# Normalised tiles in halves over both PSUM banks, with scale, shift and the first MLP matmul in units of their own

## The reference

```
def block(x, cond):                       # six times: attn, mlp, mlp, mlp, attn, mlp
    xn = (x - mean) * rsqrt(var + eps)    # over 128 features
    xm = xn * scale(cond) + shift(cond)
    y = attention(xm)  or  gelu(xm @ W1 + b1) @ W2
    return x + gate(cond) * (y + bias)
```

## Time and profile before

| | us |
|---|---|
| median of 3 runs | 586.82 (585.61 to 589.59) |
| profiled execution, whole | 584.34 |
| profiled execution, span from first to last instruction | 582.6 |
| PE busy in the span | 490.1 |
| DVE busy | 460.5 |
| ACT busy | 367.5 |
| POOL busy | 316.2 |

### The profile page before, as it was taken

One profiled execution on the slowest core, in us unless ns is written; L12 is line 12 of the kernel. 1 busy time (PEld: TensorE's weight loads), 2 busy tenths in 40 slices (PEclk: granted clock), 3 DMA queues, 4 the chain that ended last, 5 costly groups with the idle time before them and its releaser, 6 DMA issues.

```text
span 582.6 us, 23163 instructions
## 1 busy us (share of the span) xinstructions
PE 490.1 (84%) x10086; PEld 340.5 (58%) x10086; DVE 460.5 (79%) x1091; ACT 367.5 (63%) x598; POOL 316.2 (54%) x326
## 2 busy tenths in 40 slices
PE   4798658879889889689999898756889999887997
PEld 1465545656466565556667566544658666565755
DVE  5689798987886657989989876769988677899941
ACT  5865325754596759758868656522577468966652
POOL 4877356643463654685676546444353767834150
PEclk9989868898799896999999999675999999997899
DMA  8723411240232432525425413130132344422130
GB/s 293 304 89 100 125 24 35 48 120 3 74 94 60 123 96 85 135 76 151 124 78 136 105 31 84 37 98 4 24 95 72 84 128 118 115 59 61 50 97 37
DMA packets 40117, 53.51 MB, mean 92 GB/s; under 512 B 5840, under 2 KB 30672, under 8 KB 40016
## 3 DMA queue, kind: packets, MB, share of 16 engines
q1 hardware_dynamic: 39552, 51.14, 31.1%
q10 hardware_dynamic: 432, 0.88, 0.4%
q0 software_dynamic: 32, 0.01, 0.3%
HBM read 39.68 MB, written 2.88 MB: 73 GB/s over the span
## 4 chain that ended last, share of the span: by engine, by line
PE 48%; DVE 23%; issue 11%; POOL 10%; ACT 6%; DMA 1%; ACTq 0%; POOLq 0%; DVEq 0%
PE work L1067 10%; PE work L1058 10%; PE work L1009 8%; PE work L1024 6%; PE work L973 4%; DVE prob L862 3%; DVE stats L886 3%; PE work L976 3%; POOL xm L644 2%; PE work L981 2%; DVE mx L854 2%; DVE work L905 2%; POOL rstd L637 2%; DVE x L908 2%; DVE prob L856 2%
## 5 line engine op out<-in xcount | busy, mean ns | idle before, releaser
L736 ACT ACTIVATE xn<-x,nmr,rstd 128x128 f32<-128x128 f32 x192 | 79.0, 486 | 41.6 <-POOL nmr L639 41.4
L1058 PE MATMUL work<-xm,w_layer 128*128 128x512 f32 x176 | 94.9, 659 | 6.6 <-POOL xm L644 5.1
L1009 PE MATMUL work<-kbd,qT 32*32 32x80 f32 (+1 forms) x4096 | 73.6, 270 | 24.7 <-issue 17.2
L741 ACT ACTIVATE prob<-work,first 128x512 f32<-128x512 f32 x88 | 59.0, 686 | 50.5 <-PE work L1058 50.4
L727 ACT ACTIVATE prob<-prob 128x640 f32<-128x640 f32 (+1 forms) x64 | 57.5, 898 | 50.2 <-POOL prob L629 39.0
L1067 PEld LDWEIGHTS work<-w_layer,prob 128*128 128x128 f32 x704 | 82.0, 193 | 11.7 <-ACT prob L741 8.8
L1067 PE MATMUL work<-w_layer,prob 128*128 128x128 f32 x704 | 85.6, 279 | 3.0 <-ACT prob L741 2.9
L637 POOL TENSOR_TENSOR rstd<-veps,neg_half 128x4 f32<-128x4 f32 x48 | 48.9, 1018 | 66.2 <-DVE veps L893 66.2
L1009 PEld LDWEIGHTS work<-kbd,qT 32*32 32x32 f32 x4096 | 59.2, 110 | 42.7 <-issue 30.2
L644 POOL TENSOR_TENSOR xm<-turned_in,mod 128x512 f32<-128x512 f32 x48 | 50.7, 1058 | 54.5 <-DVE turned_in L899 54.5
L862 DVE STREAM_TRANSPOSE prob<-prob 128x1024 f32<-128x1024 f32 x64 | 77.2, 1227 | 2.5 <-ACT prob L727 2.5
(11 more groups left out here) (128 smaller groups left out, 828.6 us busy)
## 6 DMA issues: line engine op xcount, KB each, us to landing
gate<-gates SPq DMA_DIRECT2D x192, 128.0 KB, 3.3
vbd<-v_ev SPq DMA_DIRECT2D x128, 72.0 KB, 2.5
kbd<-in_adj SPq DMA_DIRECT2D x8, 704.0 KB, 6.5
turned_in<-in_x_tok SPq DMA_DIRECT2D x8, 256.0 KB, 2.9
out_x<-x SPq DMA_DIRECT2D x8, 256.0 KB, 2.1
turned_in<-in_x_feat SPq DMA_DIRECT2D x7, 256.0 KB, 4.6
w_layer<-in_weights SPq DMA_DIRECT2D x2, 768.0 KB, 14.2
prob<-in_modw SPq DMA_DIRECT2D x1, 768.0 KB, 10.9
```

Of the source, the lines that this page charges most:

```text
L736: act.activation(xn[s][:, t], x[s][:, t], ACT.Identity, scale=rstd[s][:, t:t + 1], bias=nmr[s][:, t:t + 1]).then_inc(xn_ready[s], 1)
L741: act.activation(hT[s][u], bank(s, f"h{j}.{u}"), GELU[BLOCKS[j][3]], bias=vec(HID_BIAS[j], u)).then_inc(h_ready[s], 1)
L1009: last = pe.matmul(to[:, b * GH * n:(b + 1) * GH * n], qT[s][rows_g, q * S:(q + 1) * S], kbd[s][rows_g, :, q * n:(q + 1) * n], start=(a != ...
L1058: pe.matmul(bank(s, f"h{j}.{u}"), w[UP[j]][:, 0, u * D:(u + 1) * D], xm[s][:], start=True, stop=True).then_inc(filled[s], 1)
```

## The change

HALVES = 2. The stages norm and modulate of a block become two each, numbered 2j and 2j + 1. The ACT part of a norm half makes two tiles, the PE part transposes two tiles into the first 256 columns of a bank of its own (fills xnj.0 and xnj.1, which lie in different banks of the stream, and turn the parity of the fills behind them). DVE scales 256 columns and POOL shifts 256 columns per half, with semaphores that count twice as far. The first hidden unit of an MLP block is two matmuls of 256 columns into one bank, each waiting for its half; the other units are whole. The attention's keys stage waits for both halves. What is computed is the same. All five MERGE strings are new: 48 more entries on PE, DVE, ACT and POOL, and the same number on SP. Of the strings, the first line of PE's stands here for all.

```diff
--- before.py
+++ after.py
@@ -77,6 +77,7 @@
 OUT_BIAS = ["L1_cond_bproj", "L1_cond_b2", "L2_cond_ssm_b2", "L2_cond_ff_b2", "L3_cond_proj_b", "L3_cond_fc2_b"]
 NATT = 4
 UNITS = 4
+HALVES = 2
 
 
 def by_pair(kind, a):
@@ -90,7 +91,9 @@
               ("self_out", 0),
               *by_pair("turn", 1), *by_pair("values", 1), ("divide", 1), ("graph_sum", 0), ("graph_out", 0)]
     for j, (kind, _, hidden, _) in enumerate(BLOCKS):
-        stages += [("stats", j), ("norm", j), ("modulate", j)]
+        stages += [("stats", j)]
+        for k in range(HALVES):
+            stages += [("norm", HALVES * j + k), ("modulate", HALVES * j + k)]
         if kind == "attn":
             a = ATTN_OF_BLOCK[j]
             stages += [("keys", a), ("base", j), ("vals", a), ("scores", a * PAIRS), ("softmax", a * PAIRS), ("scores", a * PAIRS + 1),
@@ -118,7 +121,7 @@
         ahead = [(*st, c + NS) for st in EDGES]
         at = own.index(("stats", NBLK - 1, c)) + 1
         own[at:at] = ahead
-        own.insert(own.index(("modulate", NBLK - 1, c)) + 1, ("next_x", 0, c))
+        own.insert(own.index(("modulate", HALVES * NBLK - 1, c)) + 1, ("next_x", 0, c))
     else:
         own.remove(("next_adj", 0, c))
     return own
@@ -150,24 +153,25 @@
     return [next(turns[int(s)]) for s in merge]
 
 MERGE = {
-    "tensor": ("001014414042420420132021030023021022201210212122011212121230230023023132323013113203022223321003"
...
+    "tensor": ("010104401404402104120310032132010131031200213103031330231030332322022112223333003010131222233210"
...
 }
 ORDERS = {engine: order(engine, merge) for engine, merge in MERGE.items()}
 
@@ -176,7 +180,7 @@
     names = ["rs", "self", "q a0", "k a0", "v a0", "S0 a0", "S1 a0", "q a1", "k a1", "v a1", "O0 a0", "O1 a0", "S0 a1", "S1 a1",
              "selfT", "O0 a1", "O1 a1"]
     for j, (kind, _, hidden, _) in enumerate(BLOCKS):
-        names.append(f"xn{j}")
+        names += [f"xn{j}.{k}" for k in range(HALVES)]
         if kind == "attn":
             a = ATTN_OF_BLOCK[j]
             names += [f"q a{a}", f"k a{a}", f"v a{a}", f"S0 a{a}", f"S1 a{a}", f"O0 a{a}", f"O1 a{a}", f"oT a{a}"]
@@ -400,6 +404,9 @@
         def by_seq(a):
             return a.rearrange("p (q n) -> p q n", n=S)
 
+        def half_seqs(a, k):
+            return by_seq(a)[:, k * NB // HALVES:(k + 1) * NB // HALVES]
+
         def keys_order(a):
             return a.rearrange("p (b t n) -> p t b n", b=BT, t=T)
 
@@ -433,7 +440,8 @@
         for j_, a_ in ATTN_OF_BLOCK.items():
             READ[f"oT a{a_}"] = (oT_ready, 2, a_ - 1)
         for j_ in range(NBLK):
-            READ[f"xn{j_}"] = (scaled, NBLK, j_ + 1)
+            for k_ in range(HALVES):
+                READ[f"xn{j_}.{k_}"] = (scaled, HALVES * NBLK, HALVES * j_ + k_ + 1)
             READ[f"y{j_}"] = (x_ready, NBLK + 1, j_ + 2)
             for u_ in range(BLOCKS[j_][2]):
                 READ[f"h{j_}.{u_}"] = (h_ready, NHID, HIDDEN_BEFORE[j_] + u_ + 1)
@@ -552,7 +560,7 @@
                     sp.wait_ge(scored[s], count(c, NATT * PAIRS, NATT * PAIRS))
                     load_adj(c + NS)
                 if kind == "next_x":
-                    sp.wait_ge(xm_ready[s], count(c, NBLK, NBLK))
+                    sp.wait_ge(xm_ready[s], count(c, 2 * NBLK, 2 * NBLK))
                     load_x(c + NS)
                 if kind == "store":
                     await_x(sp, c, NBLK)
@@ -638,10 +646,13 @@
                     pool.wait_ge(rstd_ready[s], count(c, 2 * NBLK, 2 * a + 1))
                     pool.tensor_tensor(nmr[s][:], neg_mean[s][:], rstd[s][:], ALU.mult).then_inc(rstd_ready[s], 1)
                 if kind == "modulate":
-                    pool.wait_ge(scaled[s], count(c, NBLK, a + 1))
-                    shift = mod[:, 2 * a + 1, c * NB:(c + 1) * NB].rearrange("p (t b) -> p t b", b=BT)
-                    turned_out = keys_order(xm[s][:]) if BLOCKS[a][0] == "attn" else as_seqs(xm[s][:])
-                    pool.tensor_tensor(turned_out, as_seqs(xm0[s][:]), shift.unsqueeze(3).broadcast_to([P, T, BT, S]), ALU.add
+                    j, k = divmod(a, HALVES)
+                    ts = slice(k * T // HALVES, (k + 1) * T // HALVES)
+                    shift = mod[:, 2 * j + 1, c * NB:(c + 1) * NB].rearrange("p (t b) -> p t b", b=BT)
+                    turned_out = keys_order(xm[s][:]) if BLOCKS[j][0] == "attn" else as_seqs(xm[s][:])
+                    pool.wait_ge(scaled[s], count(c, HALVES * NBLK, a + 1))
+                    pool.tensor_tensor(turned_out[:, ts], as_seqs(xm0[s][:])[:, ts],
+                                       shift[:, ts].unsqueeze(3).broadcast_to([P, T // HALVES, BT, S]), ALU.add
                                        ).then_inc(xm_ready[s], 1)
 
             for kind, a, c in ORDERS["gpsimd"]:
@@ -731,8 +742,9 @@
                     act.activation(oT[s][:], bank(s, f"oT a{att}"), ACT.Identity,
                                    bias=zero_col[:] if att == 2 else vec("L3_cond_qkv_b", 2)).then_inc(oT_ready[s], 1)
                 if kind == "norm":
-                    act.wait_ge(rstd_ready[s], count(c, 2 * NBLK, 2 * a + 2))
-                    for t in range(T):
+                    j, k = divmod(a, HALVES)
+                    act.wait_ge(rstd_ready[s], count(c, 2 * NBLK, 2 * j + 2))
+                    for t in range(k * T // HALVES, (k + 1) * T // HALVES):
                         act.activation(xn[s][:, t], x[s][:, t], ACT.Identity, scale=rstd[s][:, t:t + 1],
                                        bias=nmr[s][:, t:t + 1]).then_inc(xn_ready[s], 1)
                 if kind == "hidden":
@@ -892,11 +904,13 @@
                     dve.tensor_reduce(neg_mean[s][:], mv[EPS[a]][s][:, :, 0:1], AX_X, ALU.add, negate=True)
                     dve.tensor_reduce(veps[s][:], mv[EPS[a]][s][:, :, 1:3], AX_X, ALU.add).then_inc(veps_ready[s], 1)
                 if kind == "modulate":
-                    await_fill(dve, c, f"xn{a}")
+                    j, k = divmod(a, HALVES)
+                    await_fill(dve, c, f"xn{j}.{k}")
                     if c < NS:
-                        dve.wait_ge(mod_ready, a + 1)
-                        dve.wait_ge(mod_summed, a + 1)
-                    dve.tensor_tensor(by_seq(xm0[s][:]), by_seq(bank(s, f"xn{a}")), seqs(mod[:, 2 * a], c), ALU.mult
+                        dve.wait_ge(mod_ready, j + 1)
+                        dve.wait_ge(mod_summed, j + 1)
+                    dve.tensor_tensor(half_seqs(xm0[s][:], k), by_seq(bank(s, f"xn{j}.{k}")[:, 0:C // HALVES]),
+                                      seqs(mod[:, 2 * j], c)[:, k * NB // HALVES:(k + 1) * NB // HALVES], ALU.mult
                                       ).then_inc(scaled[s], 1)
                 if kind in ("project", "down"):
                     await_fill(dve, c, f"y{a}")
@@ -964,7 +978,7 @@
                     if a == 0:
                         pe.wait_ge(sf_ready[s], count(c, 2, 1))
                     if a >= 2:
-                        pe.wait_ge(xm_ready[s], count(c, NBLK, 1 if a == 2 else 5))
+                        pe.wait_ge(xm_ready[s], count(c, 2 * NBLK, 2 if a == 2 else 10))
                     if c < NS and a == 0:
                         pe.wait_ge(graph_loaded, 16)
                     if c < NS and a >= 2:
@@ -1030,11 +1044,13 @@
                     pe.wait_ge(sf_ready[s], count(c, 2, 2))
                     to_tokens(s, "selfT", sf_plain[s])
                 if kind == "norm":
-                    for t in range(T):
-                        pe.wait_ge(xn_ready[s], count(c, T * NBLK, T * a + t + 1))
+                    j, k = divmod(a, HALVES)
+                    n = T // HALVES
+                    for t in range(n):
+                        pe.wait_ge(xn_ready[s], count(c, T * NBLK, n * a + t + 1))
                         if t == 0:
-                            await_bank(pe, c, f"xn{a}")
-                        last = pe.transpose(bank(s, f"xn{a}")[:, t * P:(t + 1) * P], xn[s][:, t], ident[:])
+                            await_bank(pe, c, f"xn{j}.{k}")
+                        last = pe.transpose(bank(s, f"xn{j}.{k}")[:, t * P:(t + 1) * P], xn[s][:, k * n + t], ident[:])
                     last.then_inc(filled[s], 1)
                 if kind == "gather":
                     att = ATTN_OF_BLOCK[a]
@@ -1050,13 +1066,17 @@
                     last.then_inc(filled[s], 1)
                 if kind == "hidden":
                     j, u = divmod(a, UNITS)
-                    if u == 0:
-                        pe.wait_ge(xm_ready[s], count(c, NBLK, j + 1))
-                        if c < NS and j == 2:
-                            pe.wait_ge(w_loaded[2], 16)
+                    if c < NS and j == 2 and u == 0:
+                        pe.wait_ge(w_loaded[2], 16)
                     await_bank(pe, c, f"h{j}.{u}")
-                    pe.matmul(bank(s, f"h{j}.{u}"), w[UP[j]][:, 0, u * D:(u + 1) * D], xm[s][:], start=True, stop=True
-                              ).then_inc(filled[s], 1)
```

(8 more changed lines are left out.)

## The result

The changed kernel takes 609.36 us (601.26 to 610.95, 4 runs) beside 586.22 us of the kernel before (584.59 to 589.59, 4 runs). On another chip, the same kernel gave 598.08 us and 1.0208 (1.0144 to 1.0272), see e3. So it is 2 to 3% slower, outside the range of the prediction (597) on the first chip and just outside on the second.

A forecast was written before the change was run, and what follows sets the result against it. PE was taken to bound MLP stretches and DVE attention stretches. Relief of 10.8 us (8.4 to 13.1) less 2.2 for DVE and 1.6 for POOL gave -7.0, span 575.6, scaled to 579.8 us; range 567 to 597.

The forecast's parts named there:

- The order carries the relief through, and adds nothing of its own: All engines' rewritten orders, a term without a row: no cost or gain, bearing out a relief of 7.0 us.
- The count of cover: PE work between a stage and its user, both orders: norm shortfall 13.2 to 6.2 us, other hand-overs 11.7 and 11.6.
- Relief per pass, MLP: Norm path ahead of the first MLP matmul: 1.18 us sooner per pass, 4.3 us over 6 PE waits, from below.
- Relief ahead of attention: Norm path ahead of the query matmul: 0.69 us sooner per pass, 4.1 us over 6 PE waits, from below.
- Both banks must be free ... this adds no wait: PE's claim of two banks per norm: the other bank was read before the statistics could start, so nothing added.
- Cost on DVE and POOL: Half scales and shifts: 7.6 us more DVE work counting 2.2, 8.7 more POOL work counting 1.6.
- Split matmul at nothing: First hidden matmul as two of 256 columns: priced at nothing, from above 10.8 us of PE time.
- The total: Whole kernel: relief 10.8 us less 2.2 for DVE and 1.6 for POOL, net -7.0 us, 579.8 us, 1.2% below.
- The signs named ahead: Right: L644 wait under 6 us, PE busy within 2 us of 490. Wrong: softmax/turn waits up over 8, clock below 0.909.
- DVE bound: Rival: added work falls where DVE is full, in graph attention, and eats the relief; 596 us, chance 0.26.
- No change: Rival: PE's waits for the shift move to the next releaser, relief of about 4 us equals costs; 587 us, chance 0.19.

The follow-up runs named there:

- e3: The changed kernel once more, unedited, on another chip; 598.08 us, 1.0208 of the kernel before.
- e2: The kernel before, with whole tiles, in the new order (each pair of halves one entry at the second's place); 1.0487 of the kernel before.
- after: The changed kernel as first measured and profiled: halves, split first matmul and new orders against the kernel before; 609.36 us, 1.0306.
- e1: The changed kernel's halves in the order of the kernel before, each norm and modulate entry doubled; 1.0045 of the kernel before.
- e11: As e1, with the two banks of each stream exchanged, so a chunk's fills start at the other bank; 0.9988 of the kernel before.
- e8: The kernel before with some 34 us less DVE work (edge sums over one label, softmax maximum over 4 of 20 keys); 0.9851.
- e4: The changed kernel with the first hidden unit as one 512-column matmul behind both halves; 1.0305 of the kernel before.
- e12: As e11, but with halves in the four MLP blocks only, attention norms whole; 1.0001 of the kernel before.
- e7: The changed kernel with some 34 us less DVE work (edge sums over one label, maxima over 4 of 20 keys); no ratio, 589.12 to 603.40 us.
- e13: The kernel before with 90 idle matmuls put only ahead of 28 stages where PE stood idle over 0.5 us; 1.0012 of the kernel before.
- e14: The changed kernel with 87 idle matmuls ahead of 34 stages where PE stood idle over 0.5 us; 1.0152 of the kernel before.
- e16: The kernel before with 32 small fp32 matmuls (128 instructions) added at the start of PE, result overwritten; 1.0154 of the kernel before.
- e5: The changed kernel with two idle matmuls ahead of the waits of graph-layer scores and values, second four chunks; 1.0419 of the kernel before.
- e15: As e11, with 94 idle matmuls ahead of stages where PE stood idle over 0.5 us; 1.0039 of the kernel before.

## Why the prediction was wrong

By its own steps:

- **"The order carries the relief through, and adds nothing of its own": wrong, and this decided.** e2, the order alone, costs 4.9%, and after keeps 2 to 3% of it; with halves in both orders, e3 against e1, the order costs 1.6%. The count of cover that bore it out looked at PE work between two stages at its pipelined length. For the norm path with halves it was right: shortfall 13.2 to 6.2 us, and PE's wait for the shift went from 13.1 to 7.0. It says nothing of whole tiles, where e2 has 14.8 us at L1058 against 5.1. Wrong is that all else stays alike (11.7 and 11.6 us): the wait of the values for DVE's transposes doubled (7.1 to 14.1 us in e2, 14.9 in after), and the granted clock, which the count left out, fell (0.909 to 0.888 and 0.885). e2 has 5.9 us more issue time as well, but after has none. A term with no row behind it was set to nothing, and no rival had the order as a cost: both signs should have had one.
- **Relief per pass, MLP: right.** 4.3 us by PE's wait; e1 shows 3.7 (5.1 to 1.4), e11 2.7 (to 2.4), and in the new order it is 14.8 to 3.3.
- **Relief ahead of attention: wrong.** 4.1 us were counted, 6 waits at 0.69; the wait was 8.0 before, 8.6 in e1 and 8.5 in e11. The keys stage needs both halves, so that only a second half that ends sooner could help. Why it didn't in the old order, no run shows. In the new order the wait is 4.2 us with whole tiles (e2) and 3.7 with halves, so its fall there is the order's.
- **"Both banks must be free ... this adds no wait": wrong at another place.** At the norm it held. But two fills instead of one turn the parity behind them, and the row sums of the next chunk met the bank of the last block: 6.7 us in e1, none in e11. The text priced the claim of a bank and not the shift of all later ones.
- **Cost on DVE and POOL: right in the durations.** A half scale takes 413 ns (420 forecast), a half shift 615 (620). The busy time of L912 is 4.9 us above L899's (7.6 forecast) and of L654 6.8 above L644's (8.7), by the busy column, in which neighbouring ones overlap (96 x 0.413 = 39.6 us of durations, 37.3 busy). The Trainium skill's figure (VectorE: DVE Perf Modes, TRN2 errata) put the fixed part at 125 ns; from 413 and 681 ns it is 145 here. That the work is nearly free holds: e1 and e11 carry all of it and are at 1.0045 and 0.9988, and e8 gives 7.6 us of span for 33 us less DVE work, so that 5 us are worth about 1. Not foreseen was that the transposes, now in pairs, would keep PE busy longer (38.3 us before, 41.0 in e1, 39.1 in e11, 44.5 in after).
- **Split matmul at nothing: right.** 95.7 against 94.9 us busy, PE's whole busy time is the same in e3 and e4 (497.2 and 497.4), and the split saves 4.8 us of wait in the new order.
- **The total.** What the halves bring in the old order is none of the 7.0 us net, by e11 (0.9988) and e12 (1.0001). The relief of the MLP path is there, and is given back behind it: in e11 the wait of the values for L874 is 9.5 us against 7.1, and PE is busy 2.7 us longer.

The signs named ahead were the right ones. DVE scale and POOL shift came as said; PE's wait for L644 fell only to 7.0, not under 6; PE's busy time left the band of 2 us by 15.3; waits for softmax and turns rose by about 8; and the clock fell below 0.909.

Of the rivals, DVE bound (596) gave the nearest time, by luck as far as e7 and e8 tell: its mechanism isn't borne out. No change (587) describes the halves alone.

Added up, the 16.7 us of the profiled pair are PE busy time +15.3 (an estimated 12 to 14 of it at the lower clock, the rest the transposes in pairs and 0.8 in the split matmul) and idle time +1.4, in which the halves' saving (6 us at the shift) is used up by the values' wait (7.8 us). This is a sum and not yet a cause. Where fillers made PE's own work equally short in both orders (476 us in e13 and e14), the new order was still 1.4% slower, and the old order had gained nothing. So, as far as these runs tell, some 1.4% of the 2.1 to 3.1 doesn't go with PE's busy time, and no more than the rest goes with the clock.

Three things stay open. Why the clock falls with this order: the windows from 325 to 470 us differ in what work they hold (3324 and 2916 matmuls) as well as in the clock, and no run parts the two. Which waits the 1.4% are: the transposes' wait for the values is the one that doubled, but no run took it away alone; the blocks of instructions hardly count, with 26.6 us of issue time ahead of scores, values and masks in e13 and 28.4 in e14. And how much of the 1.6% that the order costs with halves is mere position, since e16 moved the time by 1.5%.

## What to carry to other kernels

Where every engine runs a hand-written order, price a new order as a change of its own, with a gain and a loss, and run it without the change that it was made for: here it cost more than halves were worth. Before reading a per cent, shift the program by some instructions and see what that alone does; here it was 1.5%. A bank rotation is a sequence: when one content becomes two, look at who meets whom in each later place, the first content of the next chunk above all. And hold PE's busy time against its idle time before looking for a wait. If busy time grew for the same matmuls, look at the granted clock and at how the matmuls are grouped, and then test whether a higher clock gives the time back: here most of it went into waits.

## What was not expected of the hardware

- The time of one program goes loosely with its granted clock from execution to execution. Seven executions of before that stand beside e5 to e8 lie between 583.21 us at 0.914 and 590.33 at 0.899; e7 has 589.12 at 0.904 and 603.4 at 0.889; after has 601.26 at 0.885 and 607.92 at 0.878. But before, beside e13 to e15, has 580.62 at 0.911 and 587.72 at 0.910. A gain below 1% can't be read from one profile of each.
- 128 further instructions at the start of PE, 3.6 us of work, moved the span by 9.4 us (e16).
- A higher clock need not give time: 0.909 to 0.936 in e13 came with 1.0012. The kernel's own matmuls took 14 us less of PE's time; the fillers that raised the clock took 28.5 us, and the waits that others set took the rest.
- Blocks of 256 instructions show as gaps of 0.4 to 3.9 us in runs of small matmuls, 28.6 us of 583 in before; other work ahead of them moves them (e16).
